# A four-layer decoder kernel: who places the row maxima, one Block for a norm and its attention, reordered weight turns, more filler products

## The chip, the cores and the metric

The kernel runs on one core of a Trainium2 chip. Its time is the device time of one execution, in microseconds (us); lower is better. Three executions are given, and their median counts.

## What is computed

Eight sequences of 256 tokens with 128 features (`x`, held transposed as 128 x 2048) go through four pre-norm layers. Each layer adds a self-attention, a cross-attention with `ctx_1024` (8 x 512 x 128) and a feed-forward part:

```python
x = x + _L0_attn_ref(_layernorm(x), ...)    # linear attention, 16 heads of 64
x = x + _L0_xattn_ref(_layernorm(x), ctx_1024, ...)   # 16 heads of 8, 512 keys
x = x + _L0_ffn_ref(_layernorm(x), ...)     # 8 experts
x = x + _L1_attn_ref(_layernorm(x), ...)    # over the batch axis, softmax_one, rope
x = x + _L1_xattn_ref(_layernorm(x), ctx_1024, ...)   # ONE head of 128, 512 keys
x = x + _L1_ffn_ref(_layernorm(x), ...)     # token shift
x = x + _L2_attn_ref(_layernorm(x), ...)    # keys only at shifts 0, 1, 2, 4 ... 128
x = x + _L2_xattn_ref(_layernorm(x), ctx_1024, ...)   # 512 keys
x = x + _L2_ffn_ref(_layernorm(x), ...)     # fake-quantised weights and inputs
x = x + _L3_attn_ref(_layernorm(x), ...)    # causal, 16 heads of 8, 256 keys
x = x + _L3_xattn_ref(_layernorm(x), ctx_1024, ...)   # causal, key mask, gate, 256 keys
x = x + _L3_ffn_ref(_layernorm(x), ...)     # 3 blocks of quantised + low-rank linears
```

## The kernel before, in words

There is no planner: each engine's order is written out by hand. A stage is a Block, with one program for each of the five engines; engines wait for one another through counted semaphores, and at the end of a Block all five meet. `decoder` (L3385) lists the stages.

**The narrow-head attentions** (`narrow_attention`, L3301) are a projection (`project`, L760) and a loop over the 8 sequences. `attend_wide` (L1201) serves the two with 512 keys, `attend_short` (L1382) the two of layer 3 with 256. Queries and keys are split in three bfloat16 parts, which GpSimd finishes (L984, semaphore `parts`). SyncE stores them to HBM (`store_parts`, L733) and loads them again as stacks, one row set for each head of a pair (`load_stacks`, L998). The loop is a pipeline: body s computes the scores of sequence s (PE), their maxima (VectorE, L1544), and at the same time the logits and the output sums of sequence s-1. The softmax subtracts the row maximum inside the logit product: the maxima are negated and split by GpSimd (L1104, L1106), turned by PE (`turn_max`, L1144, at head 3 of the next body for the second half of the heads, and at head 11 for the first half), copied to `max_rows` by ScalarE (`keep_max`, L1160, L1169), and then written by DMA into rows 49 and 50 of `q_stack` (`place`, L1059, two transfers for each half, issued by SyncE at L1063). PE waits at head 0 and head 8 for the stacks and for the placed maxima (`attend_halves`, L1172). ScalarE's work between is one Exp for each head (L1521, 16 a body), which PE's logits of two heads later wait for (L1432). GpSimd zeroes the future part of each head's probabilities (L1132), and PE's sums wait for four heads of those (L1189, L1459 and L1461).

SyncE's order is in `attend_transfers` (L1045). For 256 keys (`early`) it is: load stacks 1, place (0,0), wait for all `parts`, store the second quarter of the keys, place (0,1), store the remaining queries, then for each s: load (s,1), place (s-1,1), store more keys, load (s+1,0), place (s,0). A load of s > 1 waits for the logits that still read the buffer, for the stored queries and for its keys (L1054 to L1056). With 512 keys both places of s = 0 come after the stores.

**The two diagonal attentions**: `batch_attention` (L2023, layer 1) and `shift_attention` (L1574, layer 2) work in four units of 64 tokens. VectorE and GpSimd multiply q and k (L2050, L1618), PE sums over the features (`score`), VectorE takes the maximum and divides, PE spreads the probabilities over the features (`spread`), VectorE weighs v. Between, PE runs products whose result nobody reads (`keep_clock`, L181, each 128 x 512 bfloat16).

**Layer 1's cross-attention**: `fetch` (L3291) is a Block of its own that issues one weight load, `layer_norm` (L338) another Block, and `wide_head_attention` (L2263) a third, whose SyncE loads the context by sequence (L2300) and whose GpSimd stages the normed x (L2310).

**The quantised feed-forward** (`quantised_ffn`, L2891) ends with four `down` products of three matmuls each (L2961), each waiting for its quantised inputs; in its PE program `lora.turn` (L2869, eight matmuls, for the last feed-forward's weights) follows each of the first three.

## Time and profile before

| | us |
|---|---|
| three executions | 1624.26, 1625.39, 1627.04 (median 1625.39) |
| the profiled execution | 1619.48 |
| its span, first to last instruction | 1617.8 |
| busy: PE / VectorE / ScalarE / GpSimd | 1439.9 / 992.2 / 804.3 / 455.9 |
| mean granted TensorE clock | 0.954 of full speed |

Spans of the stages that the change touches, by the trace: batch attention from 646 us to 728, layer 1's cross-attention with its norm from 728 to about 804, shift attention from about 831 to 935, quantised feed-forward to 1239, the causal self-attention of layer 3 from 1239 to 1386, its cross-attention from about 1397 to 1548.

### The profile page before, as it was taken

Reading aid. Unit: us, or ns where it says so; the run is one execution under the profiler, and the core shown is the slowest. Engines: PE = TensorE matmul, PEld = TensorE weight load, DVE = VectorE, ACT = ScalarE, POOL = GpSimd, SP = SyncE. Lnnn points to the kernel's source line nnn. Section 1 sums busy time; section 2 is a strip of 40 time slices with the busy share of each in tenths; the row PEclk is TensorE's granted clock in tenths of the full one; section 3 lists DMA queues with packets and bytes.
Section 4 is the critical chain, followed back from the end, with each engine's and each line's share of the span. In section 5 each row is a group of like instructions: output and inputs, shape, how many; then the busy total and the mean of one; then the engine's idle time right before and its main releaser. Section 6 shows DMA issues by size and latency. Waiting matters only on the chain. (4 is left out here: it accounts for less than half of the span.)

```text
span 1617.8 us, 30013 instructions
## 1 busy us (share of the span) xinstructions
PE 1439.9 (89%) x10746; PEld 725.6 (45%) x10746; DVE 992.2 (61%) x1940; ACT 804.3 (50%) x1498; POOL 455.9 (28%) x656
## 2 busy tenths in 40 slices
PE   7998899999999999878987899899977788978887
PEld 5777634444454443536653452222334333433354
DVE  5666488888163221364557759998376667356746
ACT  4455437677633332304541054777754456445647
POOL 7111220000003567240035430000021456134531
PEclk9999999999999999979997899999986989898999
DMA  2000263221110000001000055322000431143100
GB/s 102 1 0 0 98 203 100 54 51 30 52 69 1 1 0 0 1 1 46 18 7 1 0 161 169 100 54 50 20 13 9 167 100 50 37 167 101 51 2 27
DMA packets 82393, 85.45 MB, mean 53 GB/s; under 512 B 7244, under 2 KB 67916, under 8 KB 81772
## 3 DMA queue, kind: packets, MB, share of 16 engines
q1 hardware_dynamic: 82296, 84.18, 16.9%
q8 instruction: 57, 0.93, 0.2%
q14 instruction: 40, 0.33, 0.1%
HBM read 51.06 MB, written 32.51 MB: 52 GB/s over the span
## 5 line engine op out<-in xcount | busy, mean ns | idle before, releaser
L1335 ACT ACTIVATE arena<-ps 128x1024 f32<-128x1024 f32 x256 | 261.8, 1023 | 109.4 <-PE ps L1242 108.9
L1227 PE MATMUL ps<-k_stack,q_stack 49*128 49x512 bf16 x512 | 190.6, 382 | 14.5 <-DVE small L1358 12.1
L1242 PE MATMUL ps<-q_stack,k_stack 51*128 51x256 bf16 x1024 | 189.6, 272 | 0.6 <-ACT arena L1335 0.4
L1355 DVE CUSTOM_DVE_ANT_0 small<-ps,mask_b 128x512 bf16<-128x512 f32 x256 | 168.0, 689 | 29.6 <-PE ps L1227 28.1
L1358 DVE TENSOR_REDUCE small<-ps 128x1 f32<-128x512 f32 x256 | 162.0, 685 | 15.9 <-PE ps L1227 14.9
L1544 DVE TENSOR_REDUCE small<-ps 128x6 f32<-128x768 f32 x128 | 122.6, 958 | 76.3 <-PE ps L1424 73.8
L1254 PE MATMUL ps<-arena,v_pad 128*32 128x256 f32 x2048 | 162.4, 391 | 1.1 <-ACT arena L1335 1.1
L1521 ACT ACTIVATE arena<-ps 128x384 f32<-128x384 f32 x256 | 118.0, 488 | 78.4 <-PE ps L1446 77.7
L1132 POOL TENSOR_SCALAR_AFFINE_SELECT arena<-arena 128x256 f32<-128x256 f32 x256 | 101.8, 406 | 86.6 <-ACT arena L1521 86.3
L2602 DVE TENSOR_TENSOR arena<-ps,arena 128x512 f32<-128x512 f32 x64 | 44.3, 692 | 101.1 <-PE ps L2519 101.0
L2676 POOL TENSOR_TENSOR arena<-arena 128x512 f32<-128x512 f32 x64 | 79.7, 1266 | 94.3 <-ACT arena L2571 94.3
L1104 POOL TENSOR_TENSOR small<-small 128x16 bf16<-128x16 f32 x64 | 13.8, 216 | 310.8 <-DVE small L1361 281.5
L1234 PE MATMUL ps<-mask_b,ident_b 64*128 64x512 bf16 x512 | 99.9, 383 | 0.5
L1227 PEld LDWEIGHTS ps<-k_stack,q_stack 49*128 49x128 bf16 x512 | 47.6, 93 | 110.9 <-DVE small L1358 80.9
L1242 PEld LDWEIGHTS ps<-q_stack,k_stack 51*128 51x128 bf16 x1024 | 75.2, 95 | 29.0 <-issue 6.8
L2565 ACT ACTIVATE arena<-ps 128x512 f32<-128x512 f32 x64 | 38.2, 597 | 90.1 <-PE ps L2515 90.1
L984 POOL TENSOR_TENSOR arena<-arena 128x512 bf16<-128x512 f32 x40 | 45.5, 1158 | 111.5 <-ACT arena L887 111.5
L2544 PE MATMUL ps<-arena 128*128 128x512 f32 x128 | 66.1, 602 | 0.7
L2515 PE MATMUL ps<-xn,arena 128*128 128x512 f32 x128 | 66.5, 601 | 0.0
L2519 PE MATMUL ps<-xn,arena 128*128 128x512 f32 x128 | 66.3, 600 | 0.0
L1254 PEld LDWEIGHTS ps<-arena,v_pad 128*32 128x32 f32 x2048 | 41.0, 108 | 55.5 <-issue 52.5
L1405 PE MATMUL ps<-mask_b,ident_b 128*128 128x256 bf16 x256 | 52.2, 287 | 14.9 <-DMA q_stack<-max_rows 14.7
(357 smaller groups left out, 2983.7 us busy)
## 6 DMA issues: line engine op xcount, KB each, us to landing
q_stack<-q_scratch SPq DMA_DIRECT2D x128, 96.0 KB
k_stack<-k_scratch SPq DMA_DIRECT2D x64, 192.0 KB
k_scratch<-arena SPq DMA_DIRECT2D x8, 768.0 KB, 3.9
k_stack<-k_scratch SPq DMA_DIRECT2D x64, 96.0 KB
q_scratch<-arena SPq DMA_DIRECT2D x4, 1152.0 KB, 7.5
arena<-in_ctxT SPq DMA_DIRECT2D x8, 512.0 KB, 6.3
k_scratch<-arena SPq DMA_DIRECT2D x8, 512.0 KB, 4.7
k_scratch<-arena SPq DMA_DIRECT2D x16, 256.0 KB, 3.8
```

Source lines behind the costliest of these rows:

```text
L1132: pool.affine_select(diag, diag, [[0, 2], [1, P]], ALU.is_ge, 0.0, 0, -1).then_inc(g["masked"].sem, 1)
L1227: pe.matmul(ps[:, t, :], c.q_stack[par][64 * e:64 * e + ROW_MAX, pr, t * P:(t + 1) * P], c.k_stack[par][64 * e:64 * e + ROW_MAX, pr, :], s ...
L1234: return pe.matmul(ps[:, 2 + 2 * (i % 2) + half, :], c.ident_b[r, :], c.mask_b[r, m:m + 2 * S], start=first, stop=False, skip_group_check= ...
L1242: mm = pe.matmul(ps[:, bank, (ch % 2) * S:(ch % 2 + 1) * S], c.k_stack[prv][64 * e:64 * e + ROWS, pr, ch * P:(ch + 1) * P], c.q_stack[prv] ...
L1254: mm = pe.matmul(ps[32 * j:32 * j + 32, 6 + grp % 2, 0:S], c.v_pad[par][:, piece, head_of(i), :], buf.probs[i % 8][:, piece * S:(piece + 1 ...
L1335: act.activation(buf.probs[i % 8], ps[:, bank:bank + 2, :].rearrange("p a n -> p (a n)"), ACT.Exp, scale=scale).then_inc(g["probs"].sem, 1)
L1355: dve.tensor_tensor_reduce(buf.junk[t], ps[:, t, :], c.mask_b[:, M_X + t * SC:M_X + (t + 1) * SC], 1.0, FLOOR, op0=ALU.add, op1=ALU.max, a ...
L1358: dve.tensor_reduce(out, ps[:, t, :], X, ALU.max).then_inc(g["maxed"].sem, 1)
L1521: act.activation(buf.probs[i % 8][:, 0:3 * P], ps[:, 4 + i % 2, 0:3 * P], ACT.Exp, scale=scale)\
L1544: dve.tensor_reduce(buf.m3[par][:, hf, :, pr % HALF, :], ps[:, bank:bank + 2, 0:3 * P].rearrange("p e (a n) -> p e a n", a=3), X, ALU.max)\
L2515: pe.matmul(ps[:, 2 + u % 2, :], w13[:, (ex * 4 + j) * P:(ex * 4 + j + 1) * P], x, start=True, stop=True)\
L2676: pool.tensor_tensor(slot(v), slot(v), share_e[v // 2 % 2], ALU.mult).then_inc(g["act_made"].sem, 1)
```

## The change

In `attend_short` ScalarE now issues the two transfers that place the maxima itself, right behind `keep_max` (a new function `place_max`); `attend_wide` leaves them to SyncE. In `attend_transfers` the stores come right after the wait for `parts`, keys before queries, for both widths, and with 256 keys the later key stores move one step ahead. The fetch, the norm and the wide-head attention become one Block; GpSimd stages the first sequence when the first norm tile is scaled and the second when all four are. In `quantised_ffn` each of the three weight turns goes ahead of the down product that it followed. The filler products go from 14 to 22 and from 12 to 20 behind the first `score`, and 12 and 14 more are run once in unit 0. `fetch` and `layer_norm` (never called any more) are deleted.

```diff
@@ -1042,6 +1020,16 @@
     body(B // 2, 0, False, True, True)
 
 
+def place_max(c, buf, eng, s, hf, par):
+
+
+    g = c.sig
+    eng.wait_ge(g["turned_out"].sem, g["turned_out"].at(s * 2 + hf + 1))
+    for e in range(2):
+        eng.dma_start(c.q_stack[par][64 * e + ROW_MAX:64 * e + ROWS, HALF * hf:HALF * hf + HALF, :],
+                      buf.maxrow[hf][8 * e:8 * e + 8, :]).then_inc(g[f"max_placed{hf}"].sem, 16)
+
+
 def attend_transfers(c, buf, sp, nk, key_mask, made):
 
 
@@ -1056,39 +1044,24 @@
             sp.wait_ge(g[f"stored_k{b // 2}"].sem, g[f"stored_k{b // 2}"].at(STORES))
         load_stacks(c, sp, b % 2, hf, b * S, b * nk, nk, b * S if key_mask else None)
 
-    def place(s, hf):
-
-        sp.wait_ge(g["turned_out"].sem, g["turned_out"].at(s * 2 + hf + 1))
-        for e in range(2):
-            sp.dma_start(c.q_stack[s % 2][64 * e + ROW_MAX:64 * e + ROWS, HALF * hf:HALF * hf + HALF, :],
-                         buf.maxrow[hf][8 * e:8 * e + 8, :]).then_inc(g[f"max_placed{hf}"].sem, 16)
+    by_sp = nk > S
 
     for hf in range(2):
         load(1, hf)
-    early = nk == S
-    if early:
-        place(0, 0)
     sp.wait_ge(g["parts"].sem, g["parts"].at(made.parts))
-    if early:
-        store_parts(c, sp, "k", nk, 1, 2, g["stored_k1"].sem)
-        place(0, 1)
+    store_parts(c, sp, "k", nk, 1, 2, g["stored_k1"].sem)
     store_parts(c, sp, "q", nk, 1, B // 2, g["stored_q"].sem)
-    if not early:
-        store_parts(c, sp, "k", nk, 1, 2, g["stored_k1"].sem)
-        place(0, 0)
-        place(0, 1)
-    for s in range(1, B + 1):
-        k = s if early else s + 1
-        if s > 1:
-            if s < B:
-                load(s, 1)
-            place(s - 1, 1)
-        if 2 <= k < 4:
-            store_parts(c, sp, "k", nk, k, k + 1, g[f"stored_k{k}"].sem)
-        if s < B - 1:
+    for s in range(B + 1):
+        if 2 <= s < B:
+            load(s, 1)
+        if s and by_sp:
+            place_max(c, buf, sp, s - 1, 1, (s - 1) % 2)
+        if s in (1, 2):
+            store_parts(c, sp, "k", nk, s + 1, s + 2, g[f"stored_k{s + 1}"].sem)
+        if 1 <= s < B - 1:
             load(s + 1, 0)
-        if s < B:
-            place(s, 0)
+        if s < B and by_sp:
+            place_max(c, buf, sp, s, 0, s % 2)
     for hf in range(2):
         sp.wait_ge(g[f"max_placed{hf}"].sem, g[f"max_placed{hf}"].at(32 * B))
 
@@ -1511,8 +1484,10 @@
             for i in range(H):
                 if back and i == 3:
                     keep_max(c, buf, act, b, 1, first)
+                    place_max(c, buf, act, b, 1, 1 - par)
                 if front and i == 11:
                     keep_max(c, buf, act, s, 0, first and par == 0)
+                    place_max(c, buf, act, s, 0, par)
                 if back:
                     act.wait_ge(g["logits"].sem, g["logits"].at(b * H + i + 1))
 
@@ -1740,7 +1715,7 @@
             pe.wait_ge(g["picks"].sem, g["picks"].at(4))
             keep_clock(c, pe, 16, bank=7)
             score(0)
-            keep_clock(c, pe, 14, bank=7)
+            keep_clock(c, pe, 22, bank=7)
             for u in range(NU):
                 spread(u, 0)
                 spread_own(u)
@@ -1748,6 +1723,8 @@
                     spread(0, 1)
                 if u + 1 < NU:
                     score(u + 1)
+                if u == 0:
+                    keep_clock(c, pe, 12, bank=7)
                 if u:
                     out_start(u - 1)
                     spread(u, 1)
@@ -2147,7 +2124,7 @@
 
             keep_clock(c, pe, 14, bank=7)
             score(0)
-            keep_clock(c, pe, 12, bank=7)
+            keep_clock(c, pe, 20, bank=7)
             for u in range(NU):
                 spread(u, 0)
                 if u == 0:
@@ -2155,6 +2132,8 @@
                 if u == NU - 1:
                     out_start(u - 1)
                 spread(u, 1)
+                if u == 0:
+                    keep_clock(c, pe, 14, bank=7)
                 if u + 2 < NU:
                     score(u + 2)
                 if 0 < u < NU - 1:
@@ -2260,7 +2239,7 @@
               spread=2 * NU, residual=NU, out_proj=NU, probs=NU, max_raw=NU, summed=2 * NU, recip=NU)
 
 
-def wide_head_attention(c, slot):
+def wide_head_attention(c, slot, name):
 
 
     nc, g, ps = c.nc, c.sig, c.ps
@@ -2275,7 +2254,8 @@
     pr = [cv.f32(2, SC) for _ in range(2)]
     pT = cv.f32(nch, S)
     sm = c.small
-    mx, nb, sums, rec = (fold(sm[:, 4 * i:4 * i + 4], (2, 2)) for i in range(4))
+    mx, nb, sums, rec = (fold(sm[:, 32 + 4 * i:36 + 4 * i], (2, 2)) for i in range(4))
+    norm = Norm(c, cv, mean=(4, 5, 6, 7), var=(2, 3, 2, 3), spread=(4, 5, 6, 7))
     SCALE = D ** -0.5
 
     def steps(engine, body):
@@ -2298,12 +2278,16 @@
 
                         wait_counted(c, sp, g["v_proj"].sem, g["v_proj"].at(b - 1))
                     sp.dma_start(csrc[par][:, :], c.io["ctxT"][:, bass.ds(at, SC)]).then_inc(g[f"src_in{par}"].sem, 16)
+            load_weights(c, sp, slot, name)
             pairs(nc, ENG.SP, body)
 
         @block.gpsimd
         def _(pool):
             def body(it):
                 for par in range(2):
+                    if isinstance(it, int):
+
+                        pool.wait_ge(g["ln_scaled"].sem, g["ln_scaled"].at(3 * par + 1))
                     b = it * 2 + par
                     if not isinstance(it, int):
                         pool.wait_ge(g["v_proj"].sem, g["v_proj"].at(b - 1))
@@ -2312,8 +2296,6 @@
 
         @block.tensor
         def _(pe):
-            pe.wait_ge(g[f"loaded{slot}"].sem, g[f"loaded{slot}"].at(16))
-
             def step(it, par, front, back):
                 first = isinstance(it, int) and it == 0 and par == 0
                 second = isinstance(it, int) and it == 0 and par == 1
@@ -2338,6 +2320,9 @@
                                        w[:, W_V:W_V + P], start=True, stop=True)
                     mm.then_inc(g["v_proj"].sem, 1)
                 if back:
+                    if second:
+
+                        pe.wait_ge(g["ln_scaled"].sem, g["ln_scaled"].at(4))
                     for t in range(2):
                         pe.wait_ge(g["normed"].sem, g["normed"].at(b * 2 + t + 1))
                         if not second:
@@ -2362,6 +2347,8 @@
                     for ch in range(nch):
                         mm = pe.matmul(ps[:, 7, 0:S], v[prv][:, ch, :], pT[:, ch, :], start=(ch == 0), stop=(ch == nch - 1))
                     mm.then_inc(g["summed"].sem, 1)
+            norm_pe(norm, pe)
+            pe.wait_ge(g[f"loaded{slot}"].sem, g[f"loaded{slot}"].at(16))
             steps(ENG.PE, step)
 
         @block.scalar
@@ -2390,6 +2377,8 @@
                         act.wait_ge(g["maxed"].sem, g["maxed"].at(s * 2 + t + 1))
                         act.activation(pr[par][:, t, :], ps[:, 3 + t, :], ACT.Exp, bias=nb[:, par, t:t + 1], scale=SCALE,
                                        accum_out=sums[:, par, t:t + 1]).then_inc(g["probs"].sem, 1)
+            norm_act(norm, act)
+            act.wait_ge(g[f"loaded{slot}"].sem, g[f"loaded{slot}"].at(16))
             steps(ENG.Activation, step)
 
         @block.vector
@@ -2419,7 +2408,10 @@
                         dve.wait_ge(g["recip"].sem, g["recip"].at(s * 2 + t + 1))
                         dve.tensor_scalar(pr[par][:, t, :], pr[par][:, t, :], rec[:, par, t:t + 1], None, ALU.mult)\
                            .then_inc(g["normed"].sem, 1)
+            norm_dve(norm, dve)
+            dve.wait_ge(g[f"loaded{slot}"].sem, g[f"loaded{slot}"].at(16))
             steps(ENG.DVE, step)
+    norm.advance()
     g.advance(staged=B, q_proj=B, k_proj=B, v_proj=B, q_kept=B, k_kept=B, v_kept=B, normed=2 * B, turned=2 * B,
               turned_out=2 * B, probs=2 * B, scores=2 * B, residual=B, summed=B, max_raw=2 * B, maxed=2 * B, recip=2 * B,
               src_in0=16 * B // 2, src_in1=16 * B // 2)
@@ -2976,9 +2968,9 @@
         pe.wait_ge(g["lora_kept"].sem, g["lora_kept"].at(2))
         pe.transpose(ps[:, 7, 0:P], amax[:, 2:3].to_broadcast([P, P]), c.ident[:, :]).then_inc(g["max_turned"].sem, 1)
         for t in range(NTI):
+            if t < NB:
+                lora.turn(pe, t, 4 + t)
             down(t)
-            if t < NTI - 1:
-                lora.turn(pe, t, 4 + t)
 
     def scalar(act):
         def round_weights(i):
@@ -3389,9 +3371,7 @@
         run(c, narrow_attention(c, 0, "w_l0x", ctx_keys=SC, mask="given"))
         combine_into(c, 0, experts(c))
         batch_attention(c)
-        fetch(c, 0, "w_l1x")
-        layer_norm(c)
-        wide_head_attention(c, 0)
+        wide_head_attention(c, 0, "w_l1x")
         token_shift_ffn(c)
         shift_attention(c, 1, "w_l2a")
         run(c, narrow_attention(c, 0, "w_l2x", ctx_keys=SC))
```

## Rows read from the trace of the kernel before

**Rows 1.** Windows of low TensorE clock: length, busy (instructions) of PE, PEld, DVE, ACT, POOL, granted clock, DMA share, GB/s
```profile
692.00:696.00 4.00, 4.00 (x21) 1.42 (x20) 2.31 (x4) 0.00 (x0) 1.86 (x2) 0.50 0.00 0
868.00:877.00 9.00, 9.00 (x58) 5.08 (x57) 6.58 (x9) 0.00 (x0) 0.61 (x1) 0.50 0.00 0
744.00:748.00 4.00, 3.93 (x12) 2.75 (x13) 0.00 (x0) 1.52 (x3) 0.00 (x0) 0.57 0.02 9
1295.00:1303.00 8.00, 8.00 (x73) 2.92 (x72) 3.40 (x5) 3.78 (x10) 2.75 (x7) 0.50 0.40 132
```
**Rows 2.** Timeline of the batch attention's first units, PE and POOL
```profile
674.85 1.93 PE L2111 MATMUL ps<-arena,consts 128*32 128x128 f32 x16
676.70 2.77 PE L186 MATMUL ps<-mask_b,ident_b 128*128 128x512 bf16 x12
681.99 1.44 PE L2124 MATMUL ps<-arena,consts 32*128 32x128 f32 x8 [2.52 <-DVE arena L2218]
683.90 3.00 PE L2111 MATMUL ps<-arena,consts 128*32 128x128 f32 x16
...
691.78 0.58 PE L2106 MATMUL ps<-mask_b,ident_b 128*128 128x512 bf16 x1 [3.81 <-DVE arena L2050]
...
686.98 4.70 POOL L2050 TENSOR_TENSOR arena<-arena 128x768 f32<-128x768 f32 x3 [6.41 <-PE ps L2111]
```
**Rows 3.** Timeline of the shift attention's first units, PE and DVE
```profile
866.46 1.16 PE L1715 MATMUL ps<-arena,consts 32*128 32x384 f32 x8 [2.17 <-DVE arena L1811]
...
877.48 0.76 DVE L1794 TENSOR_REDUCE small<-ps 128x64 f32<-128x576 f32 x1 [2.71 <-PE ps L1693]
```
**Rows 4.** Timeline of the start of the wide-head attention, PE and ACT
```profile
744.07 1.12 PE L2328 MATMUL ps<-arena,att_w 128*128 128x256 f32 x2 [3.89 <-DMA arena<-in_ctxT]
...
749.98 0.69 ACT L2391 ACTIVATE arena<-ps,small 128x512 f32<-128x512 f32 x1 [1.06 <-DVE small L2409]
```
**Rows 5.** Timeline of the end of the quantised feed-forward, PE
```profile
1224.71 1.51 PE L2961 MATMUL ps<-arena 128*128 128x512 bf16 x3 [3.97 <-POOL arena L3156]
1226.01 0.63 PE L2878 MATMUL ps<-arena 128*128 128x128 f32 x2
...
1228.74 1.46 PE L2961 MATMUL ps<-arena 128*128 128x512 bf16 x3
```
**Rows 6.** Timeline of layer 3's attentions: SyncE's queue, then PE at body 2
```profile
1281.02 2.02 SPq L744 DMA_DIRECT2D q_scratch<-arena  x3
1290.15 0.33 SPq L1004 DMA_DIRECT2D q_stack<-q_scratch  x1
...
1291.98 1.27 SPq L1063 DMA_DIRECT2D q_stack<-max_rows  x2
...
1294.49 0.61 PE L1405 MATMUL ps<-mask_b,ident_b 128*128 128x256 bf16 x2 [6.16 <-DMA q_stack<-max_rows]
...
1457.91 0.61 PE L1405 MATMUL ps<-mask_b,ident_b 128*128 128x256 bf16 x2 [7.29 <-DMA q_stack<-max_rows]
```
**Rows 7.** Timeline of one steady body: ACT and SyncE around a kept maximum, PE's sums behind it
```profile
1306.68 0.37 ACT L1169 ACTIVATE max_rows<-ps 16x256 bf16<-16x256 bf16 x1 [0.62 <-PE ps L1155]
1306.96 0.46 ACT L1521 ACTIVATE arena<-ps 128x384 f32<-128x384 f32 x1
...
1307.08 1.27 SPq L1063 DMA_DIRECT2D q_stack<-max_rows  x2
...
1308.02 0.64 PE L1459 MATMUL ps<-arena,v_pad 128*32 128x256 f32 x8
...
1307.49 0.41 POOL L1132 TENSOR_SCALAR_AFFINE_SELECT arena<-arena 128x256 f32<-128x256 f32 x1 [0.95 <-ACT arena L1521]
...
1314.36 0.64 PE L1459 MATMUL ps<-arena,v_pad 128*32 128x256 f32 x8 [0.24 <-issue]
```
**Rows 8.** Timeline, PE's turns of the maxima at head 11 of two bodies
```profile
1306.28 0.27 PE L1155 MATMUL ps<-ident_b,small 128*16 128x128 bf16 x2 [0.75 <-POOL small L1106]
...
1318.79 0.27 PE L1155 MATMUL ps<-ident_b,small 128*16 128x128 bf16 x2 [0.52 <-POOL small L1106]
```

More of the change, by code:

```diff
@@ L335, in norm_dve @@
         norm.scale(dve, t)
-def layer_norm(c, padded=None):
-    norm = Norm(c, Carver(c), padded=padded)
-    with c.nc.Block() as block:
-        @block.tensor
-        def _(pe):
-            norm_pe(norm, pe)
-        @block.scalar
-        def _(act):
-            norm_act(norm, act)
-        @block.vector
-        def _(dve):
-            norm_dve(norm, dve)
-    norm.advance()
 class FirstLoads:
@@ L3288, in lora_ffn @@
     return Program(sync, tensor, scalar, vector, gpsimd, advance, norm=norm)
-def fetch(c, slot, name):
-    with c.nc.Block() as block:
-        @block.sync
-        def _(sp):
-            load_weights(c, sp, slot, name)
 def narrow_attention(c, slot, name, ctx_keys=0, mask=None, key_mask=False, begun=False, gated=False):
```

## The prediction

> **What bounds the kernel now.** I read the clock and the stage windows first, then the timeline of the five places that the change touches, then SyncE's queue there. PE is the busiest engine by far, but nothing is near a common limit: each stage is a chain that passes from engine to engine, so each edit is priced in its own stage. In four of the five places PE runs at half clock, granted 0.50 to 0.57, right after an idle stretch of its own [rows 1]. In the two attentions of layer 3, PE stands still at body 2 for 6.16 and 7.29 us, waiting for maxima that SyncE placed late, because SyncE was itself waiting for the stored queries [rows 6]. In their steady bodies PE, ScalarE and GpSimd alternate with almost no slack [rows 7].
>
> **Batch attention, filler products.** Twelve fillers end at 679.47 (2.77 us, 0.23 each); the division releases PE at 681.99, after 2.52 idle [rows 2]. Eight more end near 681.3, so they delay nothing. Behind the gap the clock is 0.5: the same sixteen score products take 3.00 us against 1.93 at full clock [rows 2]. At full clock mask, spread and score save about 1.5 us. GpSimd's next products (4.70 us) start with that score, and their end releases score 2 after 3.81 idle [rows 2]; the 14 fillers there (3.2 us at full clock) fit in. Score 2 then runs at full clock too, where a whole 4 us window was at 0.50 [rows 1], about 1.7 us. Sum -3.2 us, bounds -6 (later clock drops vanish too) and +3 (the clock falls anyway: 14 fillers at 0.46 us are 6.4, 2.6 more than the idle 3.81).
>
> **Shift attention, the same.** PE idles 2.17 us before the first spread [rows 3]; eight fillers (1.85) fit. VectorE then waits 2.71 us for a score at 0.50 clock [rows 3, 1]; that wait is what full clock can give, -2.5. The 12 fillers (2.8 us) lie in PE's wait for VectorE's division behind it. Bounds -5 and +2.
>
> **One Block.** Before, the context load is issued only after the norm's Block, and PE's first projection waits 3.89 us for it [rows 4]. Now weights and context are loaded behind the norm, and PE goes on at 740.2, since staging sequence 0 needs the first tile alone. The projections then run without the clock drop (0.57 in that window [rows 1]; the first one took 1.12 us), for which I take 1.5 of the 1.8 us that half of the 4.0 us window holds. The bodies keep their pace from the first Exp at 749.98 [rows 4] on, so the gain stays. With 0.3 for one Block end less: -5.7, bounds -3.9 and -7. SyncE's added weight load stands in front of two context loads and hides behind 11 us of norm.
>
> **Weight turns first.** PE idles 3.97 us before the first down product, for GpSimd's clip [rows 5]. A turn takes 2.7 us (1226.01 to 1228.74 [rows 5]) and its inputs are long ready, so the first one disappears in that gap; the others only swap places with their down products. -2.7, bounds -2.7 and 0. ScalarE keeps the turned weights after its twelve roundings either way.
>
> **Placement, what is gained.** SyncE issued the query store at 1281.02 behind two placements and was free of its landing only at 1290.15; then came four loads, then the placement at 1291.98, and PE went on at 1294.49 [rows 6]. Now the stores follow the loads directly, some 6 us earlier, and the maximum needs no SyncE: both waits go, -13.4. Next late are the stacks of sequence 2: stored about 6 us earlier, loaded in 1.9 us and landed 2.5 later they come about when PE does; I charge 0.5. PE then also keeps its clock: from 1294.49 to the turn at 1306.28 (11 heads at 0.50 for most of it) are 11.8 us, while a full body of 16 heads takes 12.5, so 8.6 for 11 [rows 8, 1]. That is 3.2 for each attention, -6.4. Together -19.3. In the wide attentions, where SyncE still places, the stores only swap, long before their readers: 0.
>
> **Placement, what it costs.** No row shows ScalarE issuing a DMA. The nearest is SyncE's own pair: 1.27 us, and it starts when the copy has ended, at 1307.08, 0.40 after its start [rows 7]. On ScalarE the Exp of the next head is queued behind that pair. It began at 1306.96, 0.28 behind the copy, and would begin at 1308.35: 1.39 later [rows 7]. GpSimd's zeroing follows the Exp (1307.49 to 1307.90) and PE's sums follow that at once (1308.02 [rows 7]), so at head 11 PE loses the full 1.39. At head 3 the sums started at 1314.36, some 0.2 after their input, so 1.39 becomes about 1.1. PE leads all other chains, so nothing wins it back. Each attention has 7 such places at head 11 (sequence 0 has no logits yet) and 8 at head 3: 9.7 + 9.0 = 18.7, twice: +37.4. From below: if ScalarE's issue cost nothing, the Exp would still wait for its own copy's end, 0.12 later, +2. From above: 0.44 to 0.64 more where both queues issue at once, +10 in all. I take the row, because it is the same transfer.
>
> The Trainium skill (DMA: Bandwidth & Descriptors, Issuing engines are not separate DMA queues) says that issuing from several engines saves only sequencer time to initiate, usually small beside the transfer. Here 1.27 us of issue stands against 1.2 us from its end to PE's release at body 2 [rows 6], so it is not small, and the time saved on SyncE is paid on ScalarE. Were it small, the sum would be the first rival's.
>
> **Sum.** -3.2 - 2.5 - 5.7 - 2.7 - 19.3 + 37.4 = +4.0 us against the profiled execution's 1619.48 (span 1617.8 and 1.7 around it). That execution lies 5.9 under the median, so I carry the difference over: 1625.39 + 4.0, about 1629. About 0.2% (3.3 us) is what a measurement here can tell from no change, so this is barely slower. The sign hangs on one price: the 33.4 us of gains are used up once the Exp comes 1.2 us late, an issue of 0.55 each instead of 0.635.
>
> **Rivals.**
> 1. ScalarE issues cheaply, 0.05 to 0.3 us each: the Exp comes 0.2 to 0.7 late, +3 to +18 instead of +37, total -30 to -15, near 1603. For it: SyncE's own price varies with the form (0.33 for one load, 0.64 for this [rows 6, 7]). Against: the same transfer. Chance 0.30.
> 2. The stalls take the clock too. At head 11 PE idles 0.75 before the turn [rows 8], works about 1.3 us, then would stand for 1.4. In batch attention the clock fell after idle stretches of 2.5 and 3.8 us split by short work [rows 2, 1], and in layer 3 it stayed low for over 8 us of work [rows 1]. Each fall costs up to 3.2 us; six or so over the two attentions give +16 on top, 1645. Against: idles of 0.75 in each body leave the clock alone now. Chance 0.22.
> 3. Fillers run at half clock and hold score 2 back, +2.6 and +2 instead of -5.7: total +14, 1639. Chance 0.06.
>
> **How the numbers follow.** The forecast has 0.42, and its own range is -4 to +12 around no change's 1625 (clock phases and the bounds above): of it 0.10 is faster, 0.14 within 0.2%, 0.18 slower. With rival 1 faster is 0.40, same 0.14, slower 0.18 + 0.22 + 0.06 = 0.46. The range 1601 to 1649 leaves out the cheapest issue, at the lower end, and many clock falls at the upper; alone, the forecast would have 1621 to 1638.
>
> **What would show it.** ScalarE rows with DMA issues, and their time; the Exp behind a kept maximum starting 1.4 us later; PE idle before the sums of heads 5 and 13; body length 15 instead of 12.5 us; no 6 and 7 us waits at body 2. The first wide-head projection near PE's last norm product; clock 1.00 through the first units of both diagonal attentions; the first turn inside the wait for the clip. Wrong if bodies of layer 3 keep 12.5 us, or if the clock in them falls to 0.50.

## The result and the profile after

The changed kernel takes 1692.26 us (median of 4 runs, 1691.68 to 1698.21) against 1624.83 (1623.83 to 1627.04) of the kernel before on the same chip: ratio 1.042, interval 1.0396 to 1.0447. Of all kernels here only fast runs count, so one run of the last one (1613.9 us, over 1.5% above that kernel's fastest) is left out. The forecast was 1629, with a range up to 1649. The direction held the largest chance, but the size was missed by 63 us.

The profiled execution has a span of 1690.3 us, 72.5 more than before. It is found again stage by stage; each stretch runs between two instructions that both kernels have (mostly from start to start), so what happened earlier cancels out.

| stretch | before | after | difference | forecast |
|---|---|---|---|---|
| batch attention, first score to last residual | 52.8 | 49.2 | -3.6 | -3.2 |
| from there to the last Exp of the wide-head attention | 67.1 | 60.8 | -6.3 | -5.7 |
| shift attention, first spread to last | 60.0 | 59.7 | -0.3 | -2.5 |
| quantised ffn, first down product to last | 12.8 | 10.1 | -2.7 | -2.7 |
| layer 3, from that last down product to the last sum | 309.8 | 390.4 | +80.6 | +18.1 |

These make +67.7 us; the other 4.8 lie in stretches that the change does not touch, 3.8 of them ahead of the first combine, where the granted clock had a mean of 0.98 after and 1.00 before. The -0.3 of the shift attention has no sure sign: in the kernels below that leave this part as the change has it, the same stretch takes 57 to 61 us. The end of the page's second part shows where to look: the granted clock of the last 40th parts, 6 to 7 tenths where layer 3's attentions are.

```profile
span 1690.3 us, 30102 instructions
...
PEclk8999999999999999899988999999696667966688
```

**ScalarE's issue.** Timelines of ScalarE and PE at head 11 of one body (start, duration, what ended the idle time before). Before, the Exp behind a kept maximum began 0.28 us after the copy did [rows 7].

```profile
1310.64 0.37 ACT L1142 ACTIVATE max_rows<-ps 16x256 bf16<-16x256 bf16 x1 [0.18 <-PE ps L1128]
1311.04 1.27 ACTq L1029 DMA_DIRECT2D q_stack<-max_rows  x2
1312.49 0.87 ACT L1496 ACTIVATE arena<-ps 128x384 f32<-128x384 f32 x2 [1.48 <-PE ps L1419]
```
```profile
1311.61 0.22 PE L1419 MATMUL ps<-q_stack,k_stack 51*128 51x128 bf16 x1
1313.03 0.23 PE L1395 MATMUL ps<-k_stack,q_stack 49*128 49x128 bf16 x1 [1.21 <-ACT arena L1496]
...
1313.78 0.64 PE L1432 MATMUL ps<-arena,v_pad 128*32 128x256 f32 x8 [0.41 <-POOL arena L1105]
...
1315.70 0.61 PE L1378 MATMUL ps<-mask_b,ident_b 128*128 128x256 bf16 x2
```

The pair of issues takes the 1.27 us that SyncE's row had shown. The Exp starts 1.85 us behind the copy, 1.57 late (1.39 was forecast; 0.18 more lie between the issue's end and the Exp). PE stands 1.21 us, goes on at full clock, and some 2.7 us later its mask products take 0.61 in place of 0.39 us: the clock has fallen (0.54 from 1315 to 1317).

**The clock.** Five bodies, from one kept maximum to the same one five sequences later, were 63.3 us long before, 12.7 each. The window of before, then those of after (length; busy time and instructions of PE, PEld, DVE, ACT, POOL; granted clock; DMA share; GB/s):

```profile
1306.60:1369.90 63.30, 54.61 (x744) 21.93 (x740) 45.62 (x80) 41.43 (x100) 37.46 (x105) 1.00 0.24 71
```
```profile
1266.00:1272.00 6.00, 1.14 (x10) 0.43 (x8) 2.41 (x6) 0.00 (x0) 0.43 (x2) 0.90 1.03 394
1272.00:1276.00 4.00, 3.81 (x28) 1.35 (x28) 1.68 (x2) 1.61 (x4) 1.19 (x3) 0.50 0.03 7
...
1301.90:1394.20 92.30, 78.17 (x748) 26.77 (x748) 45.91 (x80) 41.03 (x102) 37.36 (x105) 0.67 0.14 40
```

A body takes 18.5 us, not 12.7 and not the 15 of the forecast. ScalarE, VectorE and GpSimd did the same work as before in it; PE's busy time grew from 54.6 to 78.2 us for the same products, because the granted clock had a mean of 0.67, which is half clock for two thirds of the time. The second attention shows the same: 93.6 us for five bodies at 0.65.

**The waits for maxima did not go.** PE's waits in layer 3 (total, times, longest):

```profile
PE ps L1395 <- ACT arena L1496: 29.3, 28, 1.7
PE ps L1378 <- DMA q_stack<-max_rows: 8.6, 2, 5.1
```

The 6.16 and 7.29 us at body 2 [rows 6] are gone, and two new waits stand at body 1. Timelines of SyncE, ScalarE and PE there:

```profile
1261.86 2.22 SPq L722 DMA_DIRECT2D q_scratch<-arena  x3
1264.13 3.83 SPq L722 DMA_DIRECT2D k_scratch<-arena  x3
```
```profile
1265.24 2.02 ACTq L1029 DMA_DIRECT2D q_stack<-max_rows  x2
```
```profile
1272.19 0.58 PE L1378 MATMUL ps<-mask_b,ident_b 128*128 128x256 bf16 x2 [5.05 <-DMA q_stack<-max_rows]
```

SyncE, which no longer waits for a maximum, issued three groups of stores from 1260.30 on, the next keys' too, before or while ScalarE issued the first placement. They move at 394 GB/s until 1272 (window above), and only then does PE have the maximum, two transfers of 4 KB. The two experiments with stores by pairs test this reading.

**The other stages.** The first wide-head projection follows PE's last norm product at once, and its first Exp starts at 742.25 in place of 749.98 [rows 4]. Counted from the end of batch attention's last residual (726.9 and 728.3) that is 15.3 in place of 21.7 us.

```profile
736.00 2.03 PE L207 MATMUL ps<-ident,small 128*128 128x128 f32 x16
737.87 0.60 PE L2310 MATMUL ps<-arena,att_w 128*128 128x256 f32 x2
```
```profile
742.25 0.69 ACT L2378 ACTIVATE arena<-ps,small 128x512 f32<-128x512 f32 x1 [0.90 <-DVE small L2398]
```

In batch attention the first three groups of score products run at clock 1.00. The clock falls behind a wait of 1.78 us at 698, ahead of the second unit's second spread, and the fourth group takes 3.44 us (before, 3.64):

```profile
684.18 1.14 PE L2101 MATMUL ps<-arena,consts 32*128 32x128 f32 x8 [0.80 <-DVE arena L2197]
...
692.76 1.92 PE L2088 MATMUL ps<-arena,consts 128*32 128x128 f32 x16
...
698.06 2.09 PE L2101 MATMUL ps<-arena,consts 32*128 32x128 f32 x8 [1.78 <-DVE arena L2205]
...
701.05 3.44 PE L2088 MATMUL ps<-arena,consts 128*32 128x128 f32 x16
```

The first weight turn lies inside the wait for the clip:

```profile
1211.19 0.64 PE L2870 MATMUL ps<-arena 128*128 128x128 f32 x2
...
1215.36 1.51 PE L2953 MATMUL ps<-arena 128*128 128x512 bf16 x3 [1.37 <-POOL arena L3148]
```

In shift attention the fillers filled their gap, but a second wait of 1.69 us for VectorE stood behind it, and the score after that one ran at 0.50 as before. The twelve new fillers come behind the score that they should have sped up:

```profile
857.93 2.00 PE L1677 MATMUL ps<-arena 128*128 128x64 f32 x16
861.62 1.66 PE L1690 MATMUL ps<-arena,consts 32*128 32x384 f32 x8 [1.69 <-DVE arena L1802]
863.21 0.66 PE L1663 MATMUL ps<-mask_b,ident_b 128*128 128x288 bf16 x2
863.80 4.07 PE L1668 MATMUL ps<-arena,consts 128*32 128x288 f32 x32
867.80 2.84 PE L186 MATMUL ps<-mask_b,ident_b 128*128 128x512 bf16 x12
873.31 1.14 PE L1690 MATMUL ps<-arena,consts 32*128 32x512 f32 x8 [2.67 <-DVE arena L1788]
```

### The profile page after: what moved, and what is told of

It reads as the page before. It is cut to its first block and busy times, and to the rows that moved or that the text cites. A ratio compares the mean times of both kernels' runs of the same rounds, so it can differ in the third digit from the quotient of the medians.

```text
span 1690.3 us, 30102 instructions
## 1 busy us (share of the span) xinstructions
PE 1513.9 (90%) x10788; PEld 741.1 (44%) x10788; DVE 992.7 (59%) x1940; ACT 803.1 (48%) x1498; POOL 455.6 (27%) x656
## 5 line engine op out<-in xcount | busy, mean ns | idle before, releaser
L1215 PE MATMUL ps<-q_stack,k_stack 51*128 51x256 bf16 x1024 | 189.6, 272 | 0.5 <-ACT arena L1308 0.4
L2668 POOL TENSOR_TENSOR arena<-arena 128x512 f32<-128x512 f32 x64 | 79.6, 1265 | 92.6 <-ACT arena L2563 92.6
L1395 PE MATMUL ps<-k_stack,q_stack 49*128 49x128 bf16 x256 | 63.5, 262 | 29.3 <-ACT arena L1496 29.3
L1417 PE MATMUL ps<-q_stack,k_stack 51*128 51x256 bf16 x256 | 82.7, 357 | 2.1 <-ACT arena L1496 2.0
L1397 PE MATMUL ps<-k_stack,q_stack 49*128 49x256 bf16 x256 | 80.5, 350 | 0.0
L2557 ACT ACTIVATE arena<-ps 128x512 f32<-128x512 f32 x64 | 38.1, 597 | 88.5 <-PE ps L2507 88.5
L1378 PE MATMUL ps<-mask_b,ident_b 128*128 128x256 bf16 x256 | 67.1, 358 | 8.6 <-DMA q_stack<-max_rows 8.6
L186 PE MATMUL ps<-mask_b,ident_b 128*128 128x512 bf16 x244 | 67.0, 391 | 5.3 <-DMA k_stack<-k_scratch 3.7
```

The source lines that it names most:

```text
L1215: mm = pe.matmul(ps[:, bank, (ch % 2) * S:(ch % 2 + 1) * S], c.k_stack[prv][64 * e:64 * e + ROWS, pr, ch * P:(ch + 1) * P], c.q_stack[prv] ...
L1397: mm = pe.matmul(ps[:, bank, P:3 * P], q[:, P:S], k[:, 0:S], start=False, stop=True, skip_group_check=True)
L1417: pe.matmul(ps[:, bank, 0:S], k[:, 0:P], q, start=True, stop=True, skip_group_check=True)
```

## The experiments

Eleven kernels. Ratios are to the kernel before, timed beside each; they compare better than the medians, since that kernel's own median lay between 1623.8 and 1628.2 us. "Layer 3" is the last stretch of the table above: 309.8 us before, 390.4 after. It and every window come from the one profiled execution of a kernel.

### SyncE places again, the other edits stay

```diff
-    by_sp = nk > S
+    by_sp = True
...
-                    place_max(c, buf, act, b, 1, 1 - par)
...
-                    place_max(c, buf, act, s, 0, par)
```

> The changed kernel with one part taken back: SyncE places the maxima in the two attentions of layer 3 again (the stores keep their new order, ahead of all placements). Theory A (ScalarE's issue of 1.27 to 1.30 us stops the next Exp, PE stands 1.2 us for it, its granted clock falls to 0.50, and a pair of bodies' half grows from 12.5 to 18.4 us): with the issue gone the bodies return to 12.5 us at clock 1.00, and the time is that of before less what the other four edits gained in the trace (batch attention 3.5, wide-head 6.4, weight turns 2.7, shift attention 0.3: 13), near 1612; if the earlier stores gain as well, down to 1600. Theory B (the loss comes from the new order of the stores: the first maximum now lands behind 192 KB stores, PE waits 5.05 us for it, and the bodies never find their rhythm): stays above 1660.

Measured: 1614.7 us, ratio 0.992 (0.989 to 0.996). Layer 3 takes 307.8 us. Windows over three bodies, and PE's wait for maxima:

```profile
1307.40:1345.20 37.80, 32.71 (x448) 13.15 (x444) 27.33 (x48) 24.83 (x60) 22.47 (x64) 1.00 0.24 66
```
```profile
PE ps L1378 <- DMA q_stack<-max_rows: 9.4, 2, 6.1
```

12.6 us a body, clock 1.00. Over five bodies it is 64.7 us at 0.97, in both attentions, 1.4 more than before: the clock can dip here too. Theory A holds, B falls: the whole loss hangs on the engine that places. The earlier stores, with everything else in the stretch, are worth 2.0 us, since the wait has only moved: 9.4 us in two waits are left.

### The placement alone, on the kernel before

```diff
+                    place_max(c, buf, act, b, 1, 1 - par)
...
+                    place_max(c, buf, act, s, 0, par)
```
with `attend_transfers` as the change has it.

> The kernel before with the placement edit alone (ScalarE places in the attentions of layer 3, stores in the new order); the other four edits are left out. Theory A: the changed kernel's loss in layer 3 (83 us from the first score to the end, span 1690.3 against 1617.8 with 10.7 gained ahead of it) is all here: 1625 + 80 = 1705, range 1695 to 1715, slower than the changed kernel by the 13 us of the other edits. Rival (the edits ahead of it leave PE's clock or the buffers in another state and so make part of the loss): below 1685.

Measured: 1705.04 us, ratio 1.048 (1.043 to 1.054). Layer 3: 391.0 us. Five bodies:

```profile
1302.90:1395.50 92.60, 74.12 (x743) 26.22 (x740) 45.84 (x80) 40.98 (x102) 37.49 (x106) 0.74 0.18 53
```

The loss is all here, and the edits add up as far as can be told: 1705.0 less 1692.3 is 12.7 (10 by the ratios, each good to 4 to 9 us), and the four other stages gave 12.9 in the trace. One thing stays open: these bodies are as long as the changed kernel's (92.6 and 92.3 us), though the clock is 0.74 and not 0.67, so the time at half clock does not fix the loss by itself.

### ScalarE places, and fillers where PE stands

```diff
+                if front and back and i in (5, 13):
+                    fill(10)
                 if back:
                     logit_bank(i, b, first)
```

`fill` multiplies the identity into 128 columns of bank 0 that no score uses.

> The changed kernel, and where PE waits for the delayed Exp (ahead of the logits of heads 5 and 13) ten filler products of 128 columns go to columns that nothing uses. ScalarE still issues the placements. Theory A, with the clock apart from the issue: the issue itself costs 1.1 to 1.4 us at some 30 places (about 37 us, as forecast), the rest of the 83 us (about 50) is PE's clock at 0.50. If the fillers (about 0.6 us at full clock) keep PE busy enough, the clock stays at 1.00 in the bodies, a body takes 15 us in place of 18.4, and the time is near 1650. Rival (the stall's own length and the order of the chain make the 18.4 us, the clock follows from other waits too): the clock stays near 0.5 to 0.6 and the fillers only add up to 1 us at each of 28 places: 1692 to 1715.

Measured: 1658.13 us, ratio 1.021 (1.016 to 1.027). Layer 3: 352.3 us. Windows over five bodies, then the timelines of ScalarE and PE at head 11:

```profile
1296.80:1376.30 79.50, 62.80 (x844) 27.17 (x840) 45.66 (x80) 41.38 (x101) 36.99 (x106) 1.00 0.16 46
```
```profile
1304.46 0.37 ACT L1142 ACTIVATE max_rows<-ps 16x256 bf16<-16x256 bf16 x1 [0.26 <-PE ps L1128]
1304.86 1.27 ACTq L1029 DMA_DIRECT2D q_stack<-max_rows  x2
1306.31 0.87 ACT L1502 ACTIVATE arena<-ps 128x384 f32<-128x384 f32 x2 [1.48 <-PE ps L1423]
```
```profile
1305.58 0.73 PE L1382 MATMUL ps<-ident_b 128*128 128x128 bf16 x10
1306.85 0.23 PE L1399 MATMUL ps<-k_stack,q_stack 49*128 49x128 bf16 x1 [0.54 <-ACT arena L1502]
```

The same issue, the same late Exp, but the wait of 1.2 us is now 0.73 of work and 0.54 of idle time (0.54 to 0.96 at the places of these bodies), and the clock is 1.00 in five bodies of either attention. This parts the loss in two. With the clock held, a body costs 15.9 - 12.7 = 3.2 us for its two issues, 1.6 each: the 1.57 by which the Exp is late. The clock takes the other 18.5 - 15.9 = 2.6. Over the layer: 352.3 - 307.8 = 44.5 us of issue, 390.4 - 352.3 = 38.1 of clock. The ratios give 47 and 34.

### Only the first three placements by ScalarE

```diff
+                    if first:
+                        place_max(...)
...
-        if s and by_sp:
+        if s and (by_sp or s > 1):
```
and the same for `s < B`.

> The changed kernel, but ScalarE issues only the first three placements of each attention (both of sequence 0, the first of sequence 1), while SyncE issues the other thirteen. SyncE stores early and no placement waits behind its wait for the stored queries. Theory A: ScalarE has no Exp queued behind the first placement and costs 1.3 us at most behind the next two, bodies from the second on run at 12.5 us; the 6 to 7 us waits at body 2 go, but the 5.05 us wait of the first maximum behind the stores stays: 1595 to 1612. Theory B (the store order does the harm): above 1640, with half clock from body 1 on.

Measured: 1619.97 us, ratio 0.998 (0.995 to 1.000): a miss, 8 us above the expected band. Layer 3 takes 309.8 us:

```profile
PE ps L1378 <- DMA q_stack<-max_rows: 9.3, 2, 4.8
...
PE ps L1395 <- ACT arena L1498: 4.2, 4, 1.2
```

Four waits for a late Exp are left, 4.2 us in all, and the maxima still land late, 4.5 and 4.8 us at the first placement of each attention. Together this leaves layer 3 as long as before. What the early stores alone are worth with ScalarE placing is not shown. Theory B is not borne out either, since the later bodies keep 12.6 us.

### Empty work on ScalarE instead of the issue

```diff
-                    place_max(c, buf, act, s, 0, par)
+                    empty(act, 2 * s, first and par == 0)
```

and the same at head 3; `empty` is two activations of 1x512, and SyncE places.

> The kernel of the first experiment (SyncE places), with two activations of 512 elements on ScalarE behind each kept maximum, which nobody reads: about 0.6 us each, as 128x512 activations take in the profile, so ScalarE is held about as long as by the two issues (1.27 us) but issues no transfer. Theory A (what costs is that ScalarE's next Exp is late, nothing else): bodies of 17 to 18.5 us, clock at 0.50 in them, 1614.7 + 70 to 85, so 1685 to 1700. Rival (ScalarE's own DMA queue is the harm: the placement lands later from it, or its transfers hold up SyncE's loads): the time stays below 1650, as the delayed Exp alone is partly hidden.

Measured: 1670.06 us, ratio 1.023 (1.017 to 1.028). ScalarE's timeline, and the windows of five bodies:

```profile
1304.63 1.27 ACT L1479 ACTIVATE small<-mask_b 1x512 bf16<-1x512 bf16 x2
1305.81 0.83 ACT L1502 ACTIVATE arena<-ps 128x384 f32<-128x384 f32 x2
```
```profile
1304.40:1387.20 82.80, 66.66 (x747) 24.34 (x748) 45.82 (x80) 51.26 (x121) 37.16 (x106) 0.84 0.16 44
```

The time lies between the two bands. Layer 3 takes 359.1 us: no transfer leaves ScalarE, and still 51.3 of the 82.6 us are there, so the rival falls as the main cause: a late Exp costs without ScalarE's DMA queue. Here the Exp is 1.18 us late and not 1.57, which fits the smaller loss but was not tested apart. Nor does the same delay always take the clock: five bodies of the second attention take 76.3 us at 0.96, against 82.8 at 0.84 in the first.

### Half the placements by ScalarE

```diff
-                    place_max(c, buf, act, s, 0, par)
...
-        if s < B and by_sp:
+        if s < B:
```

> The changed kernel with half the dose: ScalarE issues the placement at head 3 (second half of the heads), SyncE the one at head 11. Issue alone costs 1.6 us at each of 15 places (bodies of 15.9 against 12.65 us in the experiment with fillers), 24 us over the first experiment's 1614.7. Theory A1 (every stall of 1.2 us takes the clock for some 5 us of work, so the clock costs by the stall too): half of the 78 us, 1650 to 1658. Theory A2 (the clock falls only where two stalls follow each other within a body, 8 heads apart): only the issue, 1636 to 1641. Theory A3 (one stall per body is enough to keep it low in the whole body): above 1662.

Measured: 1663.19 us, ratio 1.020 (1.015 to 1.026), which is 1657 on the 1624.8 of before. Five bodies:

```profile
1300.10:1378.20 78.10, 65.21 (x743) 24.52 (x740) 45.73 (x80) 41.18 (x101) 36.87 (x104) 0.83 0.16 47
```

15.6 us a body: 2.96 more than before, half of the 5.80 that two placements cost. In the second attention it is 16.0 at 0.82, and layer 3 takes 356.4 us, 48.6 of the 82.6. A2 falls. A3 would need a clock that stays low; it is 0.83 here and 0.67 with both. The median lies a little above A1's band: half the placements cost half or somewhat more, so A1 holds roughly.

### The two issues of a pair two heads apart

```diff
+                if back and i in (3, 5):
+                    place_max(c, buf, act, b, 1, 1 - par, ((i - 3) // 2,))
+                if front and i in (11, 13):
+                    place_max(c, buf, act, s, 0, par, ((i - 11) // 2,))
```

> The changed kernel with the two issues of a placement parted: one behind the kept maximum, the other two heads later, so that each Exp comes at most 0.64 us late, twice as often. Theory A (a stall counts for the clock by its length: idle stretches of 0.75 us leave it at 1.00 in the kernel before, those of 1.2 to 1.4 us don't): the clock stays at 1.00, each of 60 issues costs PE 0.64 us less what a head's slack takes up, 15 to 35 us over the first experiment: 1630 to 1650. Rival (the sum of idle time counts, however it is cut): the clock falls as before, 1680 to 1700.

Measured: 1653.25 us, ratio 1.013 (1.007 to 1.019). Five bodies, and the waits for the Exp:

```profile
1308.40:1383.20 74.80, 58.94 (x732) 22.44 (x728) 44.91 (x79) 42.34 (x102) 37.20 (x105) 0.95 0.15 44
```
```profile
PE ps L1395 <- ACT arena L1498: 15.6, 25, 0.9
```

No wait for an Exp is longer than 0.9 us, yet the time misses the band by 3 us, and this window flatters it: it begins behind a fall. From the first attention's first kept maximum to its last (1264.9 to 1383.1) the clock is 0.86, in the second 0.84, and five bodies there take 78.2 us at 0.87. So short stalls keep more of the clock than the pairs (0.67 and 0.65) but not all of it; the rival, a fall as before, falls too. And the issues hide in little: two bodies at clock 1.00 (1338.9 to 1368.2) take 14.65 us each, 2.0 more than before for four issues of 0.62. Layer 3 takes 348.6 us.

### Stores by pairs of sequences, SyncE places

```diff
-    store_parts(c, sp, "q", nk, 1, B // 2, g["stored_q"].sem)
+    store_parts(c, sp, "q", nk, 1, 2, g["stored_k1"].sem)
...
+        if s == 0 and nk == S:
+            for which in "kq":
+                store_parts(c, sp, which, nk, 2, 3, g["stored_k2"].sem)
```
(the third pair at body 2; a stack load waits for its own pair's stores)

> The kernel of the first experiment (SyncE places every maximum, the four other edits stay), and the stores of layer 3's attentions cut by pairs of sequences: ahead of the first placement only keys and queries of sequences 2 and 3, then the placement, then the next pair, the last pair at body 2. Nothing waits for all queries any more. In the first experiment PE still stood 9.4 us for maxima (6.1 the longest) behind some 3 MB of stores that moved at 404 to 421 GB/s. Theory (the wait is only a place in the DMA queue): 0.77 MB take 1.9 us, so the first maximum lands within about 1 us of when it would alone, both waits go, and with them some 5 us of half clock: 10 to 15 us less than the first experiment, 1600 to 1605. Rival (the maximum's landing itself, the stack loads or the second pair of stores are what is late): 1612 to 1618, with the wait moved to another place.

Measured: 1608.13 us, ratio 0.985 (0.981 to 0.989). Layer 3: 304.5 us.

```profile
PE ps L1385 <- DMA q_stack<-max_rows: 5.4, 4, 2.5
```

The waits fall from 9.4 to 5.4 us, and the first one of the first attention to 0.62. The gain is 3.3 us in layer 3's stretch, smaller than expected; part of the wait stays (2.52 and 2.01 us in the second attention), the 2.52 where the placement stands behind two stores in SyncE's queue, and the clock falls to 0.50 behind both, for 8 us behind the second. By the ratios the gain is 12 us; the trace does not show where the rest is.

### Fillers at the waits of the shift attention

```diff
+                if u:
+                    pe.wait_ge(g["own_weighted"].sem, g["own_weighted"].at(u))
+                    keep_clock(c, pe, 10, bank=7 if u == 1 else ZB)
                 spread(u, 0)
                 spread_own(u)
                 if u == 0:
+                    keep_clock(c, pe, 7, bank=7)
                     spread(0, 1)
```

> The kernel with stores by pairs, and in the shift attention fillers where PE waits, not behind it: seven ahead of the second spread of unit 0 (PE stood 1.69 us there in the changed kernel, and its clock fell to 0.50 for the 4.07 us score behind it), ten ahead of the first spread of units 1 to 3 (waits of 2.67, 2.86 and 2.45 us, each with 0.50 behind it). The twelve fillers of the edit stay. Theory (the edit's fillers only moved the fall: they stand behind the score that they should have sped up): unit 0's score takes 2.6 in place of 4.07 us, units 1 to 3 run at 1.00, and the shift attention's 59.7 us from first to last spread become 54 to 58; total 2 to 6 us below the stores by pairs. Rival (VectorE sets the pace of the units, PE's clock doesn't): the fillers keep the clock at 1.00 and the stretch stays at 59 to 60 us.

Measured: 1596.64 us, ratio 0.981 (0.977 to 0.985). From first to last spread 51.2 us, not 59.7. PE's timeline in unit 0:

```profile
860.50 1.67 PE L186 MATMUL ps<-mask_b,ident_b 128*128 128x512 bf16 x6
862.36 0.93 PE L1695 MATMUL ps<-arena,consts 32*128 32x384 f32 x8 [0.18 <-DVE arena L1811]
863.49 0.42 PE L1668 MATMUL ps<-mask_b,ident_b 128*128 128x288 bf16 x2 [0.21 <-DVE arena L1598]
863.84 2.15 PE L1673 MATMUL ps<-arena,consts 128*32 128x288 f32 x32
```

The same 32 score products take 2.15 in place of 4.07 us. The stretch gains 8.5, more than expected (it should have come to 54 to 58 us). Not all went as the theory has it: unit 1's 32 score products still take 3.58 us at 0.58, behind a wait of 1.89 us for VectorE. PE's clock did set the pace where it was raised: the rival falls. The whole time's interval overlaps that of the stores by pairs; the stretch in the trace shows the gain.

### The first maximum ahead of the stores, and both together

```diff
+        if s == 0 and nk == S:
+            for which in "kq":
+                store_parts(c, sp, which, nk, 1, 2, g["stored_k1"].sem)
```

These lines stand behind the placement in SyncE's loop: the first pair's stores follow `place_max(c, buf, sp, 0, 0, 0)`, the second pair's go out at body 2, the third's at body 3.

> The kernel with stores by pairs, and SyncE places the first maximum ahead of any store; the first pair's stores follow it, the second pair's go out at body 2, the third's at body 3. In the stores by pairs PE still waited 5.4 us for maxima in 4 places (2.52 at the first one of the second attention, whose placement SyncE issued at 1429.66 behind two stores) and ran at 0.50 for 4 us behind that. Theory (the placement is late because of SyncE's queue and the bytes ahead of it): the first wait falls below 1 us, the clock stays, 2 to 5 us below the stores by pairs. Rival (the stores, now 3.3 us later, hold back the stacks of sequence 2): a wait of 1 to 4 us at body 2, total as before or up to 4 us longer.

> Both last edits together. If they are independent, their gains add up: 4 to 11 us below the stores by pairs, near 0.98 of the kernel before. If one of them fails, it equals the other one.

Measured: 1605.54 us, ratio 0.987 (0.984 to 0.991), and together with the fillers 1601.70, ratio 0.982 (0.977 to 0.987). Layer 3 takes 300.6 and 301.3 us, some 3 to 4 less than by pairs alone. The first wait for a maximum is 0.67 and 0.71 us in the two attentions of the first kernel, as the theory has it, and no wait for one is over 1.3 us; with the fillers one is 2.4. So the first maximum was late because of the bytes ahead of it. In the whole time this can't be told from no gain (in the first kernel's trace the wide-head stretch took 3 us more than elsewhere), so the sum of the two gains isn't shown. The lowest ratio is that of the kernel before these, 0.981, but the intervals of all four versions with stores by pairs overlap; all four are faster than both kernels of this case.

## Why the prediction was wrong

Two steps failed. The sum had no term for the clock that PE loses behind the new stalls (it stood among the rivals, as six falls worth 16 us); it came to 38.1 us. And "both waits go", -19.3 with the clock behind them, came to -2.0. Both errors lie on the slow side, so that the direction was right says little: it hung on +4.0 out of terms of 33 and 37, with 0.40 on faster.

- **Batch attention, one Block, weight turns** were right in place and size (-3.6, -6.3, -2.7 against -3.2, -5.7, -2.7). In batch attention the third group of score products gained full clock as forecast; the fourth stayed at half, as before.
- **Shift attention**, -2.5, came out at -0.3, which is no gain that can be told. The step took VectorE's wait of 2.71 us [rows 3] for what full clock gives back, and did not ask for PE's next wait behind the filled one. It was 1.69 us long, and the clock fell there. The experiment with fillers in that place got 8.5.
- **Placement, what is gained**, -19.3, came out at -2.0 (SyncE places, same stores). The working had "both waits go" because it followed SyncE's queue alone. The stores, moved ahead of the first placement, filled the DMA engines until 1272, and the maximum of sequence 0 landed with the last of them: 5.05 us where 6.16 had gone, with half clock behind it again. "Next late" was looked for among the stacks of sequence 2, not at the placement that the stores had been moved past.
- **Placement, what it costs**, +37.4: right in mechanism and nearly in size. The issue takes 1.27 us as SyncE's does; the Exp is 1.57 late, not 1.39; with the clock held the cost is 44.5. The 1.1 at head 3 was too low: the placement at head 3 alone, its clock included, costs half of a body's loss. Rival 1, the cheap issue, is refuted by the row. Small slips of the working change nothing: 8 x 1.1 is 8.8, not 9.0, and 0.12 us at 30 places is 3.6, not 2.
- **The stalls take the clock too**, rival 2, is what the forecast should have had in its sum, and it was undersized: "six or so" falls, +16. The price of a fall was not the fault (up to 3.2 forecast, 2.6 us a body measured) but their number: the clock is low in every body, 38.1 us in the layer. The evidence against it, idle stretches of 0.75 us that leave the clock alone [rows 8], was true of that trace and did not bear on stretches of 1.2 with 0.4 behind them; even four waits of at most 0.9 us a body took it to 0.84 to 0.86 over an attention. The rows that spoke for it (the clock falls behind two idle stretches in batch attention, and stays low for 8 us of work [rows 1, 2]) were named, but priced at six places out of thirty.

With the measured values the forecast's own sum gives -3.6 - 0.3 - 6.3 - 2.7 - 2.0 + 44.5 + 38.1 = +67.7. That it adds up is no test, since the last three terms come from the same stretch. The medians, which did not go into it, differ by 67.4; such closeness is partly luck, as the interval of the ratio alone is 4 us either way.

## What to carry to other kernels

An engine that feeds a tight chain should issue no transfer: its issue time goes into the chain almost whole, even in small pieces, while here SyncE, off the chain, issued the same transfers and the steady bodies kept their 12.6 to 12.9 us. Price each new stall twice, as the time PE stands and as the work behind it at half clock, and do it for each repetition. A filler helps where it stands ahead of the late input, so after filling one gap look for the next one; and a store moved earlier is also moved ahead of every small transfer that is issued after it, from another engine too.

## What the runs showed of the hardware

- The granted clock of PE fell to 0.50 (1.2 GHz) behind single waits of 1.2 us with 0.4 more behind them, and stayed at 1.00 (2.4 GHz) through five bodies when 0.73 of such a wait was filled.
- The same instructions can keep or lose it: with the empty work five bodies ran at 0.84 in the first attention and at 0.96 in the second.
- In five bodies of the changed kernel PE was busy for 78.2 of 92.3 us, and still had full clock only for about a third of the time.
- Between the end of a DMA issue on ScalarE and its next activation lie 0.18 us, and issue plus that gap stood in the way of an Exp in full; with the two issues parted by two heads, four of 0.62 cost a body 2.0 us.
- Two transfers of 4 KB, issued on ScalarE at 1265.24, released PE only at 1272.19, while SyncE's stores moved at 394 GB/s; with the same placement issued by SyncE ahead of the stores PE waited 0.67 us.
- In the profiles the kernels of this case, with the same code up to there, reach the first combine between 436.7 and 448.9 us, the latest at a mean clock of 0.96 and the earliest at 1.00, so differences under some 10 us between two kernels are read from a stretch of the trace, not from the span.
